# A routed expert layer behind a graph layer: who loads the first weights, which units lead, and who sums the squares at the end

## The reference

```python
x = x + gnn(layernorm(x), adj, nodemask, ...)
# the expert layer, on xn = layernorm(x):
logits = xn @ gate_w + gate_b
vals, idx = top_k(logits, 2); w = softmax(vals)
h = relu(einsum('bsh,ehf->bsef', xn, w1) + b1)        # 128 -> 256
expert_out = einsum('bsef,efh->bseh', h, w2) + b2     # 256 -> 128
y = xn + sum(w * expert_out[idx])
x = x + (y - mean(y)) / sqrt(var(y) + 1e-5) * gamma + beta
```

## Time and profile before

| | us |
|---|---|
| median of 3 runs | 462.59 (460.56, 462.59, 462.65) |
| the profiled execution, whole | 460.95 |
| its span in the profile | 459.2 |
| last scatter of the routing issued | 208.1 |
| first unit load issued by SP | 213.9 |
| first send, start of the last send | 225.4, 410.7 |
| first load of the last stage issued | 412.9 |
| first product of the last stage | 416.6 |
| last store issued | 455.6 |

### The profile page before, as it was taken

One profiled execution on the slowest core, in us unless ns is written; L12 is line 12 of the kernel. 1 busy time (PEld: TensorE's weight loads), 2 busy tenths in 40 slices (PEclk: granted clock), 3 DMA queues, 4 the chain that ended last, 5 costly groups with the idle time before them and its releaser, 6 DMA issues.

```text
span 459.2 us, 11050 instructions
## 1 busy us (share of the span) xinstructions
PE 335.4 (73%) x2259; PEld 276.0 (60%) x2259; DVE 304.1 (66%) x1482; ACT 220.8 (48%) x592; POOL 302.5 (66%) x331
## 2 busy tenths in 40 slices
PE   4678868877788764100999999989898989707891
PEld 3567757766778653100887787777777778603330
DVE  4686999999999974600476666666555556502895
ACT  3569869888999744100333333333333334401431
POOL 6520767777777777771277777777777777760565
PEclk9999989999999955555899999999999999956997
DMA  7812635545565722596767777777777775219974
GB/s 243 273 57 71 195 128 187 177 165 165 157 209 169 255 105 106 173 244 198 218 178 209 216 218 214 215 225 222 216 223 218 218 229 166 77 35 344 337 282 137
DMA packets 61682, 88.09 MB, mean 192 GB/s; under 512 B 10213, under 2 KB 40859, under 8 KB 61490
## 3 DMA queue, kind: packets, MB, share of 16 engines
q1 hardware_dynamic: 32370, 44.89, 33.1%
q0 software_dynamic: 10720, 25.32, 15.6%
q10 hardware_dynamic: 18528, 17.19, 12.7%
HBM read 55.61 MB, written 32.73 MB: 192 GB/s over the span
## 4 chain that ended last, share of the span: by engine, by line
PE 22%; DVE 20%; ACTq 15%; issue 14%; ACT 9%; DMA 5%; SPq 4%; POOL 3%; DVEq 0%; POOLq 0%
PE psum L1263 6%; ACTq L598 5%; ACTq L283 5%; PE psum L1252 4%; ACTq L282 4%; ACT hid L603 4%; ACT xn L532 3%; DMA out_dram<-xrow 3%; POOL token_y L442 3%; PE psum L1165 2%; DVE i L839 2%; PE psum L1155 2%; DVE xrow L1066 2%; SPq L333 1%; DVE xmid L759 1%
## 5 line engine op out<-in xcount | busy, mean ns | idle before, releaser
L442 POOL DMA_INDIRECT token_y<-yb,xb x143 | 142.9, 999 | 59.7 <-issue 40.6
L419 POOL DMA_INDIRECT sorted_x<-xrow,rows x128 | 123.4, 964 | 59.8 <-issue 56.1
L603 ACT ACTIVATE hid<-psum,b_sb 128x256 f32<-128x256 f32 (+1 forms) x188 | 69.2, 419 | 142.9 <-PE psum L1252 64.0
L1263 PE MATMUL psum<-w_sb,hid 128*128 x572 | 83.4, 283 | 11.3 <-ACT hid L603 10.4
L1263 PEld LDWEIGHTS psum<-w_sb,hid 128*128 128x128 f32 x572 | 74.7, 192 | 21.0 <-issue 18.2
L1252 PE MATMUL psum<-xbT,w_sb 128*128 128x256 f32 (+1 forms) x376 | 82.1, 342 | 2.5 <-DVE xbT L1016 2.3
L1025 DVE TENSOR_TENSOR yb<-psum,b_bc 128x256 f32<-128x256 f32 x94 | 33.9, 360 | 63.5 <-PE psum L1263 59.4
L1252 PEld LDWEIGHTS psum<-xbT,w_sb 128*128 128x128 f32 x376 | 58.0, 194 | 8.0 <-DVE xbT L1016 4.8
L1242 PE MATMUL psum<-ident_aug,xb 128*128 128x128 f32 x143 | 33.3, 290 | 24.0 <-DMA xb<-sorted_x 22.1
L1016 DVE COPY xbT<-psum 128x256 f32<-128x256 f32 x94 | 33.2, 353 | 23.5 <-PE psum L1242 23.4
L1030 DVE SCALAR_TENSOR_TENSOR yb<-yb,xb 128x128 f32<-128x128 f32 x143 | 46.3, 352 | 3.4
(11 more groups left out here) (166 smaller groups left out, 555.1 us busy)
## 6 DMA issues: line engine op xcount, KB each, us to landing
xb<-sorted_x SPq DMA_DIRECT2D x49, 258.0 KB
w_sb<-w_dram ACTq DMA_DIRECT2D x83, 128.0 KB
adj_in<-adj_dram SPq DMA_DIRECT2D x32, 256.0 KB
got<-token_y SPq DMA_DIRECT2D x16, 512.0 KB, 6.2
xb<-sorted_x SPq DMA_DIRECT2D x45, 129.0 KB
out_dram<-xrow ACTq DMA_DIRECT2D x16, 256.0 KB, 3.1
w_sb<-w_dram SPq DMA_DIRECT2D x27, 128.0 KB
xmid<-x_dram SPq DMA_DIRECT2D x6, 512.0 KB, 8.8
```

What stands on the lines that cost most here:

```text
L419: pool.indirect_dma_start(sorted_x, bass.IndirectOffsetOnAxis(ap=rows[:, slot, t, k:k + 1], axis=0), xrow[:, slot, k, t, :], None).then_in ...
L442: pool.indirect_dma_start(token_y, bass.IndirectOffsetOnAxis(ap=xb[:, q, t, TO:TO + 1].bitcast(I32), axis=0), yb[:, h, t, :], None, bounds ...
L603: last = act.activation(hid[:, u % RING, c, 0:n], psum[:, 2 + u % 2, c * BT:c * BT + n], ACT.Relu, bias=b1_sb[:, c, e])
L1263: last = mm(psum[:, 4 + u % 2, t * D:(t + 1) * D], hid[:, u % RING, c, t * P:(t + 1) * P], w2_sb[:, e, c * D:(c + 1) * D].rearrange("p a c ...
```

## The change

First, the 11 first weight loads move from SP's queue to ACT's, ahead of its first `relu`. Second, `ORDER` begins with two half units, then six full ones, then full and half in turn; the first steps of PE and DVE are written out so that the first half unit passes through all layers before the third unit begins. Third, in the last stage ACT squares tile by tile (four instructions of 128 columns instead of one of 512) and has each row's sum written to PSUM by the same instruction; DVE's `add_squares` goes, and `deviation` reads PSUM. Fourth, PE does spare products of 512 columns into an unused bank: one per 128 rows of each of the last eight units, each time such a unit has landed in `token_y`, and two more behind the last.

```diff
-ORDER = tuple(range(AHEAD)) + tuple(b for i in range(TAILS) for b in (AHEAD + i, FULL + i))
+LEAD = 2
+ORDER = (tuple(FULL + i for i in range(LEAD)) + tuple(range(AHEAD + LEAD))
+         + tuple(b for i in range(LEAD, TAILS) for b in (AHEAD + i, FULL + i)))
...
+        sums_v = psum[:, CBANKS + 2, 0:CRING * GT].rearrange("p (q t) -> p q t", t=GT)
+        hold_ps = psum[:, CBANKS + 3, :]
...
-            for u in range(IN_RING):
-                load_w1(sp, u)
             sp.wait_ge(filled, 16 * (EXPERTS + 1))
...
             act.wait_ge(table_done, 1)
+            for u in range(IN_RING):
+                load_w1(act, u)
             act.wait_ge(b1_in, 16)
...
             def square(g):
                 act.wait_ge(summed, g + 1)
-                if g >= 2:
-                    act.wait_ge(square_sums, g - 1)
-                act.activation(squares[:, g % 2, :, :].rearrange("p t c -> p (t c)"), psum[:, g % CBANKS, :], ACT.Square
-                               ).then_inc(squared, 1)
+                for t in range(GT):
+                    n = g * GT + t
+                    if n >= 2:
+                        act.wait_ge(square_sums, n - 1)
+                    act.activation(squares[:, t % 2, :], psum[:, g % CBANKS, t * D:(t + 1) * D], ACT.Square,
+                                   accum_out=sums_v[:, g % CRING, t:t + 1]).then_inc(square_sums, 1)
...
             def deviation(g):
                 q = g % CRING
-                act.wait_ge(square_sums, g + 1)
-                act.activation(rs3[:, q, 1, :], rs3[:, q, 0, :], ACT.Sqrt, bias=eps_t[:, :], scale=1.0 / D).then_inc(std_done, 1)
+                act.wait_ge(square_sums, (g + 1) * GT)
+                if g >= CRING:
+                    act.wait_ge(z_done, g - CRING + 1)
+                act.activation(rs3[:, q, 0, :], sums_v[:, q, :], ACT.Sqrt, bias=eps_t[:, :], scale=1.0 / D).then_inc(std_done, 1)
...
             for u in range(UNITS + 2):
+                if u == 2:
+                    unit_y(0)
                 if u < UNITS:
                     unit_x(u)
-                if u >= 2:
+                if u >= 3:
                     unit_y(u - 2)
...
-            def add_squares(g):
...
-            for g in range(GROUPS + 1):
-                if g < GROUPS:
-                    add_squares(g)
-                if g:
-                    scale(g - 1)
+            for g in range(GROUPS):
+                scale(g)
...
-            e1 = e2 = None
-            for u in range(UNITS + 2):
+            e2, e1 = expert_of(0), expert_of(1)
+            turn_x(0)
+            layer1(0)
+            turn_x(1)
+            layer1(1)
+            layer2(0, e2)
+            for u in range(2, UNITS + 2):
                 e0 = expert_of(u) if u < UNITS else None
                 if u < UNITS:
                     turn_x(u)
-                if 1 <= u <= UNITS:
+                if 3 <= u <= UNITS:
                     layer1(u - 1)
-                if u >= 2:
+                if u >= 3:
                     layer2(u - 2, e2)
...
+            def hold_clock(n):
+
+                for _ in range(n):
+                    mm(hold_ps, ident[:, :], w2_sb[:, 0:2, :].rearrange("p e c -> p (e c)"), start=True, stop=True)
+
+            for u in range(UNITS - OUT_RING, UNITS):
+                pe.wait_ge(yb_out[u % OUT_RING], 16 * sent(u, OUT_RING))
+                hold_clock(tiles_of(u))
+            hold_clock(2)
             for g in range(GROUPS):
                 add_pair(g)
```

More of the change, by code:

```diff
@@ L54 @@
 AHEAD = FULL - TAILS
-ORDER = tuple(range(AHEAD)) + tuple(b for i in range(TAILS) for b in (AHEAD + i, FULL + i))
+LEAD = 2
+ORDER = (tuple(FULL + i for i in range(LEAD)) + tuple(range(AHEAD + LEAD))
+         + tuple(b for i in range(LEAD, TAILS) for b in (AHEAD + i, FULL + i)))
+assert sorted(ORDER) == list(range(UNITS))
 IN_RING = 11
@@ L214, in build @@
         got = sb("got", [P, GOT_RING, GT, TOPK, D])
-        squares = sb("squares", [P, 2, GT, D])
-        rs3 = sb("rs3", [P, CRING, 3, GT])
+        squares = sb("squares", [P, 2, D])
+        rs3 = sb("rs3", [P, CRING, 2, GT])
         z = xrow[:, 0, :, :, :].rearrange("p k t c -> p (k t c)")[:, 0:CRING * GT * D].rearrange(
@@ L257, in build @@
         got_in = [sem(f"got_in{q}") for q in range(GOT_RING)]
-        summed, squared, square_sums, std_done, z_done, res_done = (
-            sem("summed"), sem("squared"), sem("square_sums"), sem("std_done"), sem("z_done"), sem("res_done"))
+        summed, square_sums, std_done, z_done, res_done = (
+            sem("summed"), sem("square_sums"), sem("std_done"), sem("z_done"), sem("res_done"))
         res_out = [sem(f"res_out{q}") for q in range(CRING)]
@@ L1060, in scale @@
                 dve.wait_ge(std_done, g + 1)
-                n = step(v.reciprocal(rs3[:, q, 2, :], rs3[:, q, 1, :]))
+                n = step(v.reciprocal(rs3[:, q, 1, :], rs3[:, q, 0, :]))
                 dve.wait_ge(dve_step, n)
@@ L1066, in scale @@
                     last = v.scalar_tensor_tensor(out=z[:, q, t, :], in0=psum[:, g % CBANKS, t * D:(t + 1) * D],
-                                                  scalar=rs3[:, q, 2, t:t + 1], in1=gamma_bc[:, :], op0=ALU.mult, op1=ALU.mult)
+                                                  scalar=rs3[:, q, 1, t:t + 1], in1=gamma_bc[:, :], op0=ALU.mult, op1=ALU.mult)
                 last.then_inc(z_done, 1)
-            for g in range(GROUPS + 1):
-                if g < GROUPS:
-                    add_squares(g)
-                if g:
-                    scale(g - 1)
+            for g in range(GROUPS):
+                scale(g)
         @block.tensor
```

## The result

The changed kernel took 456.75 us in the median of 4 runs (456.47 to 457.32), the kernel before on the same chip 462.20 (460.56 to 462.65): a ratio of 0.989, 95% interval 0.9863 to 0.9917. The forecast was 456.9. Run again later beside the kernel before, the same kernel gave 0.9916 (0.9883 to 0.9948). The profiled execution took 456.47 us, its span is 454.7, against 459.2 before; that difference of 4.5 is taken apart here.

What follows compares the result with a forecast made beforehand. POOL's 143 sends were taken to bound the unit stage, PE and DMA the last stage's pace. Gains of 2.5 (start), 2.0 (spare products) and 1.2 (pace) sum to 5.7: 462.59 - 5.7 = 456.9 us, range 452.5 to 461.5.

Steps and rivals of the forecast that it cites:

- Start of the units: First seam: without weight loads on SP and with half units first, third send at 225.5 instead of 228.02, gain 2.5.
- If that lands as the last send does: First seam: last scatter lands 2.09 after its issue, at 210.2, so the first unit load goes out at 211.1.
- Would put the rise near 219: First seam: PE's work begins 3.1 earlier, so its granted clock rises near 219 instead of 222 to 223.
- The lower bound of this term: Start of the units: if PE stays at half clock, the third send comes 1.0 late (-1.0).
- Spare products: Second seam: PE's clock stays at 1.00, so the last stage's first group takes 1.72 and not 3.77, gain 2.0.
- Pace: Last stage: 8 periods at 2.0 and 7 at 1.72, together 28.0 against 29.24, gain 1.2.
- DVE is no bound any more: Last stage: DVE loses one instruction per group and so does not limit the pace; no size given.
- the rest is DMA: Last stage before the change: periods are 1.95, PE alone would give 1.72, and DMA makes the difference.
- Tail: Behind the last group: ACT's four squares take 0.7 more, DVE's summing of a group goes; together nothing.
- the bound of -1.3 for the spare products: Second seam: if the clock fell anyhow, five spare products would end 3.4 late; lower bound set at -1.3.
- ACT as the bound: Rival, last stage: squares at 0.46 make a group on ACT 2.5, 15 periods 8.3 more, whole 466.4; chance 0.10.
- PE alone: Rival, last stage: PE sets all 15 periods at 1.72, 25.8 together, gain 3.4 and not 1.2, whole 454.7; chance 0.15.

Runs made afterwards that it cites:

- weights on SP: Changed kernel with the 11 first weight loads back on SP's queue; 456.06 us, ratio 0.9898.
- warm start: Changed kernel with 16 more spare products on PE right before its first unit; 456.13 us, ratio 0.9894.
- old squares: Changed kernel with squares as before the change: one of 512 columns on ACT, summed on DVE; 457.49 us, ratio 0.9925.
- spare products alone: Kernel before with PE's spare products as the only change; 457.98 us, ratio 0.9953.
- no spare products: Changed kernel with PE's spare products taken out; 458.52 us, ratio 0.9958.
- squares alone: Kernel before with the tile-by-tile squares and row sums on ACT as the only change; 460.10 us, ratio 0.9993.

## Why the prediction was right, and which of its steps were not

The time and the direction were right, and the largest single part, PE's clock at the second seam, is shown. Term by term:

**Start of the units, 2.5 forecast.** The pair of profiles gives 1.57 from the scatter to the third send, and the means of the kernels with the old start (19.11) and the new one with lead (17.96) only 1.15, all of it ahead of the first unit load (5.09 against 3.96). Part of the profile's figure is the profile before itself: its first unit load stood 5.81 behind the scatter, while two kernels with the same start had 4.71 and 4.76. Three steps failed. "If that lands as the last send does" took 2.09; the scatter took 3.10, because the weight loads that had left SP now ran beside it. "Would put the rise near 219" took the clock from where PE's work begins; it rose at 222, and the first full unit's layer 1 cost 1.76. This one is a matter of the execution: in the same kernel run again it rose at 219.6, 5.5 behind PE's first work, and in three more kernels with lead 5.7 to 6.1 behind, as forecast; in the changed kernel's first profile and with the weights on SP it took 7.3. And the third send was given 0.3 behind DVE, where every send that waits starts 0.86 to 0.88 behind (226.91 against 225.44 + 0.61), as the first one had in the earlier trace rows. The lower bound of this term, a clock that stays low, named the right danger. The lead, half of the working, is not shown to pay anywhere: with a cold clock that rises at about the same moment it is worth 0.1 to 0.2 (four kernels against four), and the 1.2 with the warm start is less than the fall of the clock cost there.

**Spare products, 2.0 forecast.** 1.74 in the first group. The 1.72 left out the 0.3 from PE's end to ACT's start that the 3.77 had in it. Granted clock 1.00 in the pauses, and the spare products done ahead of the data, as said. What the forecast lacked was a second effect: with the first group on time the loads do not stop, and the last eight periods shrink by 0.4 to 0.6 (16.65 and 16.86 against 17.22, one profile each).

**Pace, 1.2 forecast, 1.20 measured**, and split as forecast: 7 periods at 1.72 (12.01), 8 at 2.0 (16.03). But "DVE is no bound any more" had no term, and "the rest is DMA" was wrong for the end of the stage. The chain of the kernel before ends in DVE's own work:

```profile
448.75 0.60 DVE xrow L1066 x2
449.35 0.59 DVE rs L1056
...
450.59 0.60 DVE xrow L1066 x2
451.19 0.59 DVE rs L1056
...
451.90 1.14 DVE xrow L1066 x4
```

A period of 1.84 there is DVE's (450.59 - 448.75); in the chain after, PE's products stand in that place. I had read DVE's share off a window, and not followed the chain to its end.

**Tail, 0 forecast, 0.75 measured.** "DVE's summing of a group goes: nothing" set it off against ACT's four squares at 0.33. They start 0.22 to 0.25 apart, so they take 1.05 and not 1.32, and the sum of the last group had been queued behind the scaling of the group before, on the chain. Both kernels with DVE's sums and spare products have 9.57 and 9.58, all others without the sums 8.76 to 8.83.

The terms come to 4.5 in the profiles, where 5.7 was forecast. The medians differ by 5.45 in the runs of the result (four each) and by 4.2 in the later ones (6 against 15); the kernel before had 462.2 in those first four and 460.2 to 460.9 in the three later sets of 15 to 19. The good hit on the median is thus partly luck: the start was taken 0.9 to 1.4 too large and the tail 0.75 too small, and the base was high. Two slips in the working moved nothing: the bound of -1.3 for the spare products comes to -1.4 by its own terms (2.0 - 3.4), and neither it nor the -1.0 of the start went into the upper end of the range.

**The rivals.** ACT as the bound did not come: it idles 0.46 ahead of the last group's squares. The rule weighed there, from the Trainium skill (Perfetto Trace Analysis, Optimizing Scalar/DVE Operations), holds in its first half, four small instructions cost 0.45 more than one large one (1.05 against 0.60, the row sums included); the engine was not saturated, so its time of 466.4 did not come. PE alone sets the first seven periods, not the last eight.

**What stays open.** Whether a microsecond won at the start is there at the end is shown in part. In all fourteen profiles POOL waits for nothing behind the third send, as forecast: the gaps from there to the last send come to about 43.1 every time. What varies is the time of the 140 sends between, 138.7 to 141.7, and it alone makes the 181.8 to 184.8. So a gain at the third send is passed on, less what the sends take longer; why some do is open. The whole times agree. Two pairs differ by the start alone: old squares (0.9925) against spare products alone (0.9953), and no spare products (0.9958) against squares alone (0.9993). That is 1.3 and 1.6 us for the start, each about as large as its noise, both the same way. Which of the two edits of the start it is, the whole times of the runs without one of them don't show.

## What to carry to other kernels

Measure a stage from an event inside it (here the first load of the last stage): the whole time moved by a microsecond and more between executions, the stage with spare products by half of one. Only so was it seen that the squares are worth 1.6 to 1.7 with the spare products and at most 0.8 without. Keep PE busy over the wait at a seam: the late first group cost not only its own 1.7 us but held up the ring of loads, and with it the end of the stage. Before an instruction is called free because its engine has time, follow the chain to its last row. Before two kernels are compared at a seam, see whether the clock rose at the same moment in both.

## What the runs showed of the hardware

The row sum has a record of its own, in the groups on ACT (busy us, mean ns, idle before):

```profile
L626 ACT ACTIVATE squares<-psum 128x128 f32<-128x128 f32 x64 | 16.7, 310 | 27.2 <-PE psum L1299 27.2
...
L626 ACT ACTIVATION_READ_ACCUMULATOR squares<-psum 128x1 f32 x64 | 11.4, 179 | 0.0
```

It lies inside the square's own time and the next square's start, so that neither mean is the price: 0.24 from start to start is.

The granted clock held at 1.00 over pauses of PE of 1.0 to 1.1 us between spare products, and over 1.65 us with the warm start; after 3.12 us it fell to 0.50, there not during the pause but when the work had come back. In the kernel before, at the last seam, it fell in the pause itself, at 403.1 with PE without a record since 400.7.

A send that POOL waits for starts 0.86 to 0.88 us behind its releaser's end, one that is queued behind another 0.30. The store on the last stage's chain landed in 6.28 us in the changed kernel, and in 7.10 and 7.86 with the same squares but a late first group.
